# Local attention of a hybrid model: the window mask written by ScalarE instead of added by TensorE, and a new instruction order on three engines

## The reference, cut to what matters

```
def local_attention(q, k, v):          # 16 heads of 64, window 32, 256 tokens
    ...                                # each window of 32 queries sees its own 32 keys and the 32 before
    mask = (it < jb) | (it > jb + w) | (jb == -1)
    sim = jnp.einsum('bhwie,bhwje->bhwij', bq, bk2) * QK_SCALE
    sim = jnp.where(mask, -jnp.finfo(sim.dtype).max, sim)
    attn = jax.nn.softmax(sim, -1)
    out = jnp.einsum('bhwij,bhwje->bhwie', attn, bv2)

for i in range(DEPTH):                 # DEPTH = 6
    x = attn_layer(shift_tokens(x), Wqkv[i], q_scale[i], k_scale[i], Wo[i]) + x
    x = ffn_layer(shift_tokens(x), ...) + x
```

## Time and profile before

| what | value |
|---|---|
| time, median of 3 runs | 7207.77 us (7205.19 to 7207.87) |
| the profiled execution's own time | 7208.77 us |
| its span, first to last instruction | 7206.7 us |
| mean granted TensorE clock | 0.823 of full speed |
| busy: PE, PEld, DVE, ACT, POOL | 74%, 47%, 53%, 55%, 33% of the span |
| L403, the mask matmuls | 384 of them, 149.3 us busy |

### The profile page before, as it was taken

One profiled execution on the slowest core, in us unless ns is written; L12 is line 12 of the kernel. 1 busy time (PEld: TensorE's weight loads), 2 busy tenths in 40 slices (PEclk: granted clock), 3 DMA queues, 4 the chain that ended last, 5 costly groups with the idle time before them and its releaser, 6 DMA issues. The chain is left out here.

```text
span 7206.7 us, 178920 instructions
## 1 busy us (share of the span) xinstructions
PE 5312.7 (74%) x69288; PEld 3368.6 (47%) x69288; DVE 3840.9 (53%) x6202; ACT 3985.0 (55%) x8451; POOL 2396.7 (33%) x1351
## 2 busy tenths in 40 slices
PE   1000198888888888977777988888888979687778
PEld 0000065655656564733333655656564747343444
DVE  5555654645455554555554645455554546445854
ACT  4333264646455555539997646555554546355655
POOL 0000162626354444504443626354453535000000
PEclk6555599999999999976666989999998989766876
DMA  1000121212222121200000212212121212000000
GB/s 43 0 0 0 37 51 48 55 49 54 53 49 59 42 53 50 57 11 1 1 1 20 55 47 53 54 45 52 47 57 44 57 45 57 18 2 3 0 2 6
DMA packets 177838, 248.52 MB, mean 34 GB/s; under 512 B 51692, under 2 KB 79848, under 8 KB 175080
## 3 DMA queue, kind: packets, MB, share of 16 engines
q1 hardware_dynamic: 177128, 237.68, 13.2%
HBM read 43.50 MB, written 5.24 MB: 7 GB/s over the span
## 5 line engine op out<-in xcount | busy, mean ns | idle before, releaser
L377 PE MATMUL PS<-arena 128*128 128x512 f32 x2304 | 1163.5, 632 | 220.0 <-ACT arena L500 117.1
L670 POOL TENSOR_TENSOR arena<-arena 128x512 f32<-128x512 f32 x384 | 586.6, 1551 | 651.3 <-DVE arena L622 651.3
L670 POOL TENSOR_TENSOR lns<-arena 128x512 f32<-128x512 f32 x384 | 566.1, 1498 | 666.7 <-DVE arena L622 666.7
L377 PEld LDWEIGHTS PS<-arena 128*128 128x128 f32 x2304 | 412.9, 199 | 646.1 <-issue 359.7
L499 ACT ACTIVATE arena<-PS 128x512 f32<-128x512 f32 x768 | 472.1, 615 | 333.4 <-PE PS L377 258.4
L434 PE MATMUL PS<-arena 64*64 64x32 f32 x24576 | 534.7, 227 | 155.4 <-ACT arena L531 121.4
L592 DVE TENSOR_REDUCE arena<-PS 128x16 f32<-128x1024 f32 x192 | 235.2, 1225 | 731.0 <-PE PS L408 731.0
L1106 PE MATMUL PS<-arena 128*128 128x512 f32 x8 | 6.7, 1019 | 807.8 <-DVE arena L1040 807.8
L434 PEld LDWEIGHTS PS<-arena 64*64 64x64 f32 x24576 | 509.5, 141 | 191.7 <-issue 188.0
L611 DVE TENSOR_REDUCE arena<-arena 128x32 f32<-128x2048 f32 x192 | 438.8, 2285 | 293.4 <-ACT arena L500 286.1
L539 ACT ACTIVATE arena<-PS 128x512 f32<-128x512 f32 x384 | 208.9, 597 | 648.0 <-PE PS L434 648.0
(11 more groups left out here) (254 smaller groups left out, 11101.2 us busy)
## 6 DMA issues: line engine op xcount, KB each, us to landing
arena<-arena SPq DMA_DIRECT2D x2880, 64.0 KB, 2.0
arena<-in_L_ffn_Wqkv SPq DMA_DIRECT2D x12, 1536.0 KB, 6.5
arena<-in_L_ffn_Wo SPq DMA_DIRECT2D x48, 128.0 KB, 6.3
scratch<-arena SPq DMA_DIRECT2D x4, 1024.0 KB, 4.8
arena<-scratch SPq DMA_DIRECT2D x4, 1024.0 KB, 7.6
arena<-in_L_ffn_W SPq DMA_DIRECT2D x12, 341.0 KB
arena<-in_ffn_scales SPq DMA_DIRECT2D x12, 128.0 KB, 5.8
arena<-in_L_ffn_W SPq DMA_DIRECT2D x12, 128.0 KB
```

The lines of the kernel that those rows point to most:

```text
L377: pe.matmul(PS[:, QKV + n % 2, :], xs[uu % 2][:, par * P:(par + 1) * P], w, start=True, stop=True).then_inc(qkv_ready, 1)
L670: last = pool.tensor_tensor(heads(t2)[:, :, a:a + 32], heads(raws[par])[:, :, b:b + 32], sine, ALU.mult)
```

## The change

The mask is no longer added by TensorE. ScalarE writes it into the two score banks ahead of the score matmuls (`write_mask`), and two matmuls at the start of each layer set the banks up so that the later ones add to what is there. The projection chunks are issued singly in places, both halves of the scores stand before `heads`, ScalarE starts a tile with `exps`, and copies chunks 4 and 5 and computes `rnorm` after `copy_probs`. On VectorE `unit_length` moves behind `softmax_shift` and `add_stream`. The bf16 copies of identity and mask go.

```diff
             def scores(g, tt, s):
                 if s == 0:
                     wait_alone(pe, turned_copied, nth(g, TURN_PER, place_qk(tt, 3)) + 2)
-                    wait_alone(pe, scores_read, nth(g, TILES, tt))
-                mask = masks_b[:, par * 2 * WIN:(par + 1) * 2 * WIN].rearrange("p (o j) -> p o j", o=1)
-                pe.matmul(PS[:, SCORE + s, :], ident_b[:], mask.broadcast_to([P, PAIRS, 2 * WIN]),
-                          start=True, stop=False, skip_group_check=True)
+                    wait_alone(pe, mask_ready, nth(g, TILES, tt))
...
             # TensorE, body
-                    for half in range(2):
-                        if further:
-                            qkv(g, tt + 3, (2 * half, 2 * half + 1))
-                        if ahead:
-                            turn_qk(g, tt + 1, (2 * half, 2 * half + 1))
+                    if further:
+                        qkv(g, tt + 3, (0,))
+                    if ahead:
+                        turn_qk(g, tt + 1, (0,))
+                    if further:
+                        qkv(g, tt + 3, (1,))
+                    if ahead:
+                        turn_qk(g, tt + 1, (1, 2))
+                    if further:
+                        qkv(g, tt + 3, (2, 3))
+                    if ahead:
+                        turn_qk(g, tt + 1, (3,))
                     if further:
                         qkv(g, tt + 3, (4, 5))
                     turn_probs(g, tt, final)
                     if ahead:
                         scores(g, tt + 1, 0)
+                        scores(g, tt + 1, 1)
                     heads(g, tt, final)
-                    if ahead:
-                        scores(g, tt + 1, 1)
                     if tt % 2 == 1:
                         project(g, tt // 2)
             wait_alone(pe, attn_w_loaded, (run + 1) * ATTN_LOADS)
+            for s in range(2):
+                pe.matmul(PS[:, SCORE + s, :], ident[:], Wqkv[:, 0:CH], start=True, stop=True).then_inc(banks_marked, 1)
...
+            def write_mask(g, tt):
+                S = PS[:, SCORE:SCORE + 2, :].rearrange("p s (m e) -> p (s m) e", e=FD)
+                act.activation(S, masks[:, tt % 2:tt % 2 + 1, :].broadcast_to([P, FH, 2 * WIN]), ACT.Copy)\
+                   .then_inc(mask_ready, 1)
...
             # ScalarE, body
+                    exps(g, tt)
+                    if ahead:
+                        copy_turned(g, tt + 1, (0,))
                     if further:
                         copy_qkv(g, tt + 3, (0, 1), True)
-                    exps(g, tt)
                     if ahead:
-                        copy_turned(g, tt + 1, (0, 1))
+                        copy_turned(g, tt + 1, (1, 2))
                     if further:
                         copy_qkv(g, tt + 3, (2, 3), True)
                     if ahead:
-                        copy_turned(g, tt + 1, (2, 3))
+                        copy_turned(g, tt + 1, (3,))
+                        write_mask(g, tt + 1)
+                    copy_probs(g, tt, final)
+                    if further:
+                        rnorm(g, tt + 3)
+                    if tt % 2 == 0 and not (final and tt + 4 >= TILES):
+                        enter(it * UNITS_IN_BODY + (tt + 4) // 2, (tt + 4) // 2 % 2)
                     if further:
                         copy_qkv(g, tt + 3, (4, 5), True)
-                        rnorm(g, tt + 3)
-                    copy_probs(g, tt, final)
                     copy_heads(g, tt, 0)
                     copy_heads(g, tt, 1)
                     if tt % 2 == 1:
                         copy_projected(g, tt // 2)
-                    elif not (final and tt + 4 >= TILES):
-                        enter(it * UNITS_IN_BODY + (tt + 4) // 2, (tt + 4) // 2 % 2)
             first = run * BODIES
             enter(0, 0)
             enter(1, 1)
+            act.wait_ge(banks_marked, 2 * (run + 1))
+            write_mask(first, 0)
...
             # VectorE, body
                     softmax_norm(g, tt, nth(g, TURN_PER, place_probs(tt - 1, 1, False)))
-                    if not (final and tt + 3 >= TILES):
+                    if further:
                         norms(g, tt + 3)
-                        unit_length(g, tt + 3)
-                    if not (final and tt + 1 >= TILES):
+                    if ahead:
                         softmax_shift(g, tt + 1)
                     if tt % 2 == 1:
                         add_stream(g, it, tt // 2)
+                    if further:
+                        unit_length(g, tt + 3)
...
             # GpSimd, once in each of the two calls
-            pool.tensor_copy(ident_b[:], ident[:]).then_inc(masks_cast, 1)
-            pool.tensor_copy(masks_b[:], masks.rearrange("p t j -> p (t j)")).then_inc(masks_cast, 1)
```

More of the change, by code:

```diff
@@ L146, in program @@
         lns = sb("lns", N)
-        ident_b = sb("ident_b", P, BF16)
-        masks_b = sb("masks_b", 2 * 2 * WIN, BF16)
         ffn = Space(0)
@@ L224, in program @@
         probs_ready = sem("probs_ready")
-        masks_cast = sem("masks_cast")
+        mask_ready = sem("mask_ready")
+        banks_marked = sem("banks_marked")
         vw_ready = [sem(f"vw_ready{i}") for i in range(2)]
@@ L630, in body @@
                 for tt in range(TILES):
+                    ahead = not (final and tt + 1 >= TILES)
+                    further = not (final and tt + 3 >= TILES)
                     softmax_norm(g, tt, nth(g, TURN_PER, place_probs(tt - 1, 1, False)))
-                    if not (final and tt + 3 >= TILES):
+                    if further:
                         norms(g, tt + 3)
-                        unit_length(g, tt + 3)
-                    if not (final and tt + 1 >= TILES):
+                    if ahead:
                         softmax_shift(g, tt + 1)
```

## The result

The changed kernel takes 7283.85 us (7272.62 to 7301.93, 4 runs), beside 7206.48 us for the kernel before on the same chip: a ratio of 1.0109, 95% interval [1.0087, 1.0131]. It is 1.1% slower; 1.1% faster was forecast, 154 us less than it takes.

What follows compares the result with a forecast made beforehand. TensorE was taken to bound the steady tiles. Per layer 7.8 + 7.8 - 4.1 - 7.2 - 1.3 - 0.9 + 4.6 = 6.7 us, times 12 is 80: 7208.8 - 80 = 7129, given as 7130 us; 8-in-10 range 7020 to 7210.

Steps and rivals of the forecast that it cites:

- ScalarE's new order ... Cost 0: Steady tiles: ScalarE's reordered work and mask write delay nothing on TensorE, least margin 0.3 us; cost 0.
- The walk: One steady tile followed step by step on ScalarE: copies and mask (8.9 against 9.52 us) are seen before TensorE needs them.
- Fetch: Dense run of scores and `heads`: instruction-fetch pause grows from 0.45 to 1.0 us a tile; 7.2 us a layer lost.
- fetch stays as it is: Rival: pauses remain at 0.45 us a tile because the sequencer runs ahead in the slow part; 7031 us; chance 20%.
- A worse fetch: Rival: a fetch pause worse than the forecast's 1.0 us a tile, worst-case bound 1.35; chance 11%.
- The unit of 34.2 to 34.6 us: Steady stretch: two tiles would take this time in place of 35.56 us, TensorE above 95% busy.
- The mask matmuls: Steady stretch: 25 of 26 mask matmuls on TensorE fall away, 0.31 us each; 7.8 us a layer gained.
- The steady wait of `heads` for the copies: Ahead of `heads`: 13 waits of 0.68 us for copied probabilities go, 8.8 us; net 7.8 us a layer gained.
- `project` waits 96 times: `project` directly behind `heads` waits for copied heads, 0.68 us in six odd tiles; 4.1 us a layer lost.
- the prologue: Start of each layer: two 512-column matmuls cost 1.5 us, less two masks of tile 0; 0.9 us lost.
- the last three tiles: Layer's end, a chain: first step 12.6 us, gain 2.3; second 15.45, loss 1.35; sum 4.6 us a layer gained.
- the third step: From the end of tile 14's `heads` to the start of the last `heads`: 11.67 us before; 3.6 us gained.

Runs made afterwards that it cites:

- h1: Changed kernel, but VectorE writes the mask right behind the shift, over a tile ahead, in place of ScalarE; 0.9998 of the kernel before.
- h3: e7 plus about 1 us of ScalarE work that nobody reads, whose end the scores wait for; 1.0059 of the kernel before.
- e7: Changed kernel's new order, with the masks added by TensorE as before; 7207.59 us, 0.9978 of the kernel before.
- e4: Kernel before in its old order, with only the mask moved to ScalarE; 7305.76 us, 1.0151 of the kernel before.
- e8: No part of the model: TensorE alone runs small products in a straight row, then mixes with 512-column products; row mostly 3.45 us per 256 instructions.
- f1: Changed kernel with a TensorE product of zeros added to each score bank, mask still from ScalarE; 1.0063 of the kernel before.
- e1: Changed kernel with the last projection chunk of each tile placed between scores and `heads`; 7154.35 us, 0.9932 of the kernel before.
- e5: Changed kernel with 200 always-met waits ahead of TensorE's code, which moved it by 100 instructions; 7283.14 us, 1.0092 of the kernel before.
- g1: e7 with 8 always-met waits ahead of TensorE's code, a shift of 4 instructions; 0.9970 of the kernel before.
- g2: f1 with 248 always-met waits ahead of TensorE's code, a shift of 124 instructions; 1.0166 of the kernel before.
- g3: e7 with 128 always-met waits ahead of TensorE's code, a shift of 64 instructions; 0.9940 of the kernel before.

## Why the prediction was wrong

**The step that failed first is "ScalarE's new order ... Cost 0".** The walk was right as a walk: the mask was written in 1.09 us and no steady L404 is recorded as waiting for it. But I asked only whether the array would wait. The wait stands ahead of the dense run and holds TensorE's sequencer: ScalarE is done only 0.7 us before the first score, the sequencer's lead over it is 0.64 us where h1 has 1.35, and in the tile shown the next block comes 1.00 us behind the wait. An early mask (h1 against the changed kernel) is worth 0.0111 of 7210, 80 us of the 154 that were missed; adding such a wait (h3 against e7) costs 0.0081, 58 us. Whether the same cause is part of e4's loss wasn't tested.

**Fetch.** The rate was right, a block of 256 instructions in 3.2 to 3.5 us (3.45 in e8, 64 bytes each), and the case "fetch stays as it is" fell: the sequencer does run ahead of the array (by 0.64 us at the first score), and the pauses grew all the same. The size was too small: 1.0 us a tile, taken from two borders in the middle of an undisturbed run. Recorded issue pauses are 209.3 us in 203 places where 130 to 170 us stood; counted as the prediction counts, with 0.2 hidden in each, that is 1.30 a tile, where its gain of 80 us, 0.42 for each of 192 tiles, is used up at 1.42. The 0.2 is the last matmul's record less the step to the next start: the two small lines of before have records of 0.22 to 0.23 us in the mean, at steps of 0.016 (1.03/64) and 0.019 (2.46/128).

```profile
L434 PE MATMUL PS<-arena 64*64 64x32 f32 x24576 | 534.7, 227 | 155.4 <-ACT arena L531 121.4 <-issue 32.8
...
L408 PE MATMUL PS<-arena 64*32 64x64 f32 x24576 | 451.1, 218 | 31.3 <-issue 29.1
```

I worked the 1.0 out from the dense run's own speed, with the block before it always there in time. The mask's gain and this loss are perhaps also not independent, as f1's ratio suggests: time taken off TensorE next to such a border isn't gained in full (119 us of products gave 1.0063 for 1.0109). A worse fetch had a chance of 11%, and its sign is the one measured. 167.0 of the 209.3 us are in `heads`, the second half of the run.

**The clock was no term of the sum at all.** I took the granted clock of the steady tiles (0.99) as given. Behind some of the new pauses it is about half for some us (0.51 in the 4.00 us behind the 1.16, 0.54 in the 4.15 behind e1's 1.67): 61 us of TensorE's busy time in the steady tiles beyond the forecast. In h1, without the late wait, the twelve windows still sum to 2804.25 us, 2571.42 busy, so 51 us over the forecast's busy time and 25 over its idle time: 76 together, where the changed kernel has 107.5. So in the steady tiles of these two traces the early mask took away only 31 of 107.5 us, and the clock, with 51 left, is the largest term that the sum lacked. (The unit of 34.2 to 34.6 us was also too low for the prediction's own terms, which give 35.56 - 1.24 - 1.36 + 0.68 + 1.10 = 34.7.)

```profile
sum 2804.25, PE 2571.42 PEld 1958.71 DVE 1955.87 ACT 1741.73 POOL 1797.92; mean PE 214.29 PEld 163.23 DVE 162.99 ACT 145.14 POOL 149.83
```

**What held.** The mask matmuls are gone. The steady wait of `heads` for the copies is gone. `project` waits 96 times, 64.7 us, inside the 60 to 70 forecast. The first shift of the first layer starts at 916.27 in place of 915.50: 0.8 us for the prologue, 0.9 forecast. The clock there rises from 0.50 to 1.00 at 880.33, and at 881.85 before, so the two matmuls did bring that forward. No L376 waits longer for ScalarE in steady tiles, and `unit_length` and L623 (1.98 us in the median, for 1.23) stay hidden there. **In the last three tiles** only the third step came as forecast. For the first, from 1154.51 to the end of `heads` at 1169.7, 12.6 us were forecast and 15.1 measured: `turn_probs` waits for L623 until 1161.72, so 7.2 after the start, where the forecast had that product done at 6.05, and `heads` has a pause of 1.18 and a clock of 0.55 behind it. The second also missed:

```profile
1161.72 1.09 PE L417 MATMUL PS<-ident,arena 128*128 128x128 f32 x8 [2.27 <-DVE arena L623]
...
1166.70 3.15 PE L430 MATMUL PS<-arena 64*64 64x32 f32 x98 [1.18 <-issue]
1170.53 5.36 PE L442 MATMUL PS<-arena 128*128 128x256 f32 x16 [0.68 <-ACT arena L550]
1180.20 1.09 PE L417 MATMUL PS<-ident,arena 128*128 128x128 f32 x8 [0.28 <-DVE arena L623]
1181.63 1.88 PE L404 MATMUL PS<-arena 64*32 64x64 f32 x128 [0.34 <-ACT PS L535]
...
1192.31 1.97 PE L417 MATMUL PS<-ident,arena 128*128 128x128 f32 x8 [5.00 <-DVE arena L623]
1195.25 4.29 PE L430 MATMUL PS<-arena 64*64 64x32 f32 x128 [0.97 <-ACT arena L542]
```

`project` at a clock of 0.69 (5.36 for 3.57), a wait for L623 and one for the mask: 17.5 us between the two ends of `heads` in place of the 15.45 forecast. The last step has the 5.00 and the 1.97 that were forecast. Summed over the twelve layers, the three steps gained 23 us (508.5 to 485.3), where 4.6 a layer are 55; h1 gains 46 (462.4). With the 107.5 us of the steady tiles this is 139 of the 144 us by which the profiled execution missed 7129.

**What stays open.** How much of the rest after h1 is clock and how much pause, since the two replace each other; why the same pause brings the clock down in one body and not in the next; and what decides whether moving the code helps. Why `turn_probs` meets L623 later than in the walk wasn't followed either. What starts a block's transfer no run shows; the 1.00 us behind the wait was read in one tile of three kernels. The long pauses of a body stand in its first tile (1.67 in e1, 1.74 after), but no run here takes the loop away, so whether the loop has a part in them isn't shown.

## What to carry to other kernels

A wait that nobody is seen waiting for can still cost. Ahead of a dense run that pauses at every 256th instruction, have what the run waits for ready some us early: here the mask on VectorE, 7.2 to 16.9 us before the first score of a steady tile in place of 0.7, was worth 1.1%. Work taken off an engine beside such pauses may not be gained (119 us of products came back for nothing in f1); put slow instructions (a projection chunk of 512 columns) between runs of small matmuls, and look for the pair, early operands and a split run: together they gave 2.7% against the changed kernel, 1.1 and 1.8 alone. And put the clock into the sum: behind a new pause in a stretch at full clock as much again can be lost (behind the 1.67 of e1 `heads` took 4.15 in place of 2.52, at a clock of 0.54). A test that shifts code should count in the trace by how much it shifted.

## What the hardware showed that was not expected

- A straight run of small matmuls takes 3.45 us for 256 instructions, a pause of 0.94 us behind 2.52 us of work, with no transfer but the instructions' own (e8). The end of each of its 114 pauses stands 1.17 to 1.60 us behind the end of a 16 KB block's transfer.
- In the first tile of the body shown, a block's transfer starts 1.00 us after the sequencer has passed its last wait, in the kernel after, in h1 and in h3, where nobody reads the work waited for, though the array is busy with `turn_probs` meanwhile.
- A wait can hold the sequencer without any idle time of the array at that place: the sequencer's lead over the first score matmul is 0.64 us in the kernel after and 1.35 in h1 (medians of 156 tiles).
- Two waits in a row that are always met take one instruction of TensorE's code (99 in the trace for 200, e5).
- At a mean clock of 0.62 there are no pauses: 512 matmuls in 13.42 us without one, where four blocks at full clock take 13.8 with their pauses (e8).
- 384 more matmuls of 0.31 us (f1) didn't make the changed kernel slower (1.0063 for 1.0109), though they moved its code too.
- 4 to 124 instructions that do nothing, at the start of the code, changed the time by -0.4% to +1% (g1, g2, g3, e5).
- A write of 1024 f32 into PSUM took 1.09 us on ScalarE and 1.23 us on VectorE.
